# A graph network on one core: four of its five adjacency products in float32r halves, edge weights from rows in SBUF

## The reference

```python
# layer 0, three rounds: sum over neighbours, then two linear layers with batch norms
agg = segment_sum(h[src], dst); z = h + agg; z = z @ W1[i] + b1[i]; ...
# layer 1: mean over row = src, of x[col = dst]
agg = segment_sum(x[col], row) / maximum(deg, 1)
# layer 2: mean over dst, of x[src]
agg = segment_sum(x[src], dst) / clip(deg, 1); h = agg @ W_l.T + b_l + x @ W_r.T
# layer 3: weighted max and weighted mean
w = edge_weight / maximum(segment_sum(edge_weight, dst), 1e-12)[dst]
feat = relu(x @ W_pool + b_pool); neigh = segment_max(feat[src] * w[:, None], dst)
h = relu(normalise(x @ W1_self + neigh @ W1_neigh + b1))
neigh2 = segment_sum(h[src] * w[:, None], dst) / maximum(deg, 1)
out = relu(h @ W2_self + neigh2 @ W2_neigh + b2)
```

## Time and profile before

| what | value |
|---|---|
| median of 3 executions (lowest, highest) | 4459.0 us (4453.96, 4469.67) |
| span of the profiled execution | 4464.1 us |
| PE busy | 3506.4 us, 79% |
| DVE busy | 2050.4 us, 46% |
| ACT busy | 1045.6 us, 23% |
| POOL busy | 2442.1 us, 55% |
| DMA moved | 1224.69 MB |

### The profile page before, as it was taken

One profiled execution on the slowest core, in us unless ns is written; L12 is line 12 of the kernel. 1 busy time (PEld: TensorE's weight loads), 2 busy tenths in 40 slices (PEclk: granted clock), 3 DMA queues, 4 the chain that ended last, 5 costly groups with the idle time before them and its releaser, 6 DMA issues.

```text
span 4464.1 us, 71523 instructions
## 1 busy us (share of the span) xinstructions
PE 3506.4 (79%) x24839; PEld 2663.0 (60%) x24839; DVE 2050.4 (46%) x5883; ACT 1045.6 (23%) x2703; POOL 2442.1 (55%) x2510
## 2 busy tenths in 40 slices
PE   0005878564589997899889998999658998989998
PEld 0004666443457774677667775777447777777776
DVE  6533343344244456878765544000334444444445
ACT  0003555342430002000140003000333333333331
POOL 4777777777303444555404444544177777777750
PEclk9999998787889998999999999999868999999999
DMA  9999999887559999787799997666235677767765
GB/s 368 365 364 359 363 367 343 292 296 261 186 152 339 374 376 310 258 273 265 245 349 366 370 349 256 193 193 194 92 110 186 236 257 244 261 236 268 243 228 188
DMA packets 320171, 1224.69 MB, mean 274 GB/s; under 512 B 98815, under 2 KB 111392, under 8 KB 303353
## 3 DMA queue, kind: packets, MB, share of 16 engines
q1 hardware_dynamic: 143706, 705.58, 44.7%
q10 hardware_dynamic: 96287, 459.59, 27.9%
q0 software_dynamic: 79872, 55.32, 5.2%
HBM read 964.59 MB, written 337.59 MB: 292 GB/s over the span
## 4 chain that ended last, share of the span: by engine, by line
PE 36%; POOL 26%; DMA 17%; issue 12%; DVE 5%; POOLq 1%; ACT 1%; another core or an unknown queue 1%; ACTq 1%; DVEq 0%; SPq 0%
PE PS L507 28%; POOL PAN L387 18%; POOL counts L725 7%; DMA counts<-SSB 7%; DMA BB<-share_rows 6%; DMA counts<-val_slot,idx_slot 2%; PE PS L444 2%; PE PS L1430 2%; DMA PAN<-counts 1%; DVE ST L835 1%; PE PS L486 1%; DVE BB L835 1%; PE PS L450 1%; POOLq L719 1%
## 5 line engine op out<-in xcount | busy, mean ns | idle before, releaser
L751 POOL DMA_INDIRECT shares<-dst_f,spare x832 | 808.8, 972 | 1176.7 <-DMA shares<-dst_f,spare 553.6
L507 PE MATMUL PS<-PAN,HH 125*128 125x375 bf16 x8000 | 1405.7, 297 | 29.7 <-DMA PAN<-counts 15.1
L387 POOL DMA_INDIRECT PAN<-table,src_i x832 | 811.2, 975 | 351.6 <-issue 276.8
L725 POOL DMA_INDIRECT counts<-val_slot,idx_slot x832 | 809.3, 973 | 347.9 <-issue 325.8
L507 PEld LDWEIGHTS PS<-PAN,HH 125*128 125x128 bf16 x8000 | 778.2, 98 | 328.6 <-issue 23.3
L507 PE MATMUL PS<-PAN,XP 125*128 125x375 bf16 (+1 forms) x4000 | 863.1, 297 | 0.0
L444 PE MATMUL PS<-PAN,HH 125*128 125x375 bf16 x2000 | 363.1, 305 | 607.6 <-DMA PAN<-counts 607.6
L444 PEld LDWEIGHTS PS<-PAN,HH 125*128 125x128 bf16 x2000 | 180.2, 101 | 649.2 <-issue 487.8
L507 PEld LDWEIGHTS PS<-PAN,XP 125*128 125x128 bf16 x4000 | 389.2, 97 | 150.9 <-issue 1.6
L646 ACT ACTIVATE X<-PS 125x625 bf16<-125x625 bf16 x500 | 345.1, 692 | 450.1 <-PE PS L450 433.0
L872 DVE TENSOR_REDUCE X<-PAN 125x5 f32<-125x3125 bf16 x100 | 334.3, 3400 | 75.5 <-DMA PAN<-counts 75.3
(11 more groups left out here) (263 smaller groups left out, 3876.4 us busy)
## 6 DMA issues: line engine op xcount, KB each, us to landing
PAN<-counts SPq DMA_DIRECT2D x300, 800.0 KB
counts<-SSB ACTq DMA_DIRECT2D x10, 8000.0 KB, 35.9
shares<-SSB SPq DMA_DIRECT2D x50, 1600.0 KB
PAN<-counts ACTq DMA_DIRECT2D x100, 800.0 KB
shares<-blank ACTq DMA_DIRECT2D x25, 3200.0 KB, 16.9
XP<-shares SPq DMA_DIRECT2D x50, 1600.0 KB
PAN<-shares SPq DMA_DIRECT2D x50, 1600.0 KB
turned<-X ACTq DMA_DIRECT2D x100, 781.2 KB
```

The lines of the kernel that those rows point to most:

```text
L387: nc.gpsimd.indirect_dma_start(out=gbuf[g % 2][:, k, :], out_offset=None, in_=source, in_offset=bass.IndirectOffsetOnAxis(ap=src_i[:, t:t ...
L507: last = nc.tensor.matmul(dense_ps[b][h], xpart[part][0:TN, s * SUBJ + j, :], (turned_tile if scales else panel)[u % NPAN][0:TN, j, lo:lo ...
L725: nc.gpsimd.indirect_dma_start(out=counts_flat, out_offset=bass.IndirectOffsetOnAxis(ap=idx_slot[b][:, k:k + 1], axis=0), in_=val_slot[b][ ...
L751: nc.gpsimd.indirect_dma_start(out=shares_flat, out_offset=bass.IndirectOffsetOnAxis(ap=share_at[:, t:t + 1], axis=0), in_=share[:, t:t + ...
```

## The change

Products 2 to 5 take the node rows as two float32r halves (`XH`, `XL`) instead of three bf16 parts. float32r is a four-byte operand type of PE, and both operands must have it, so each panel is first cast from bf16 into one of three slots (`CX` twice, `CP`; `CB` in product 5), six panels of a chunk by ACT and four by DVE (`ON_DVE`). In product 3 ACT casts tile by tile and sums with it. SP reloads a panel's buffer when its cast is done. A panel is then 5 x 2 x 2 = 20 matmuls, of 376 and 250 columns. The weights come from keys, sources and weights that three DMAs put into SBUF once in the build, as rows with a halo of 63 (`half_key`, `half_w`), by one 127-wide product a column (`dve_share_columns`), beside the build's groups; the broadcasts and `dve_shares` are gone. The scatters no longer wait for PE; they wait once for all weights, and for each half of the edges once for the zeros. The zero slices move: 2 in each chunk of product 2, 5 behind it, none later. Not shown are the two rounds' split into halves, the casts between rows, and the names of slots.

```diff
 PART_AT = {DONE_AT[c] + 2 + d: c * NBLK + d for c in range(NBLK - 1) for d in range(NBLK)}
 ZPARTS = 5
 ZBUILT = 5
-ZEROS_AT = {"dense1": (0,) * 10, "taken1": 5, "dense2": (1,) * 10}
-WEIGH_AT = {1: (0,) + (7, 6) * 4 + (0,), 3: (6,) * 8 + (4, 0)}
+ZEROS_AT = {"dense1": (2,) * 10, "taken1": 5, "dense2": (0,) * 10}
+NCAST = 3
+ON_DVE = (1, 3, 6, 8)
+HALO = 63
+HL = T // 2
+HWIDE = HL + 2 * HALO
+LANE = -(-HL // 3)
+SHARES_FROM = 6
+SHARES_TURN = SHARES_FROM + HL // GT
+FAR = 1000.0
 BN_EPS = 1e-5
 NORM_EPS = 1e-12
 
...
+        def cast_may_start(eng, v):
+            n, u = 1 + v // (NBLK * NSUB), v % (NBLK * NSUB)
+            eng.wait_ge(panel_in[u % NPAN], 16 * (NBLK * NSUB // NPAN * n + u // NPAN + 1))
+            if v >= NCAST:
+                eng.wait_ge(panel_used, NPAN + NBLK * NSUB + v - NCAST + 1)
+
+        def act_casts(act, n, c, subs):
+
+            for s in subs:
+                if s in ON_DVE:
+                    continue
+                v = ((n - 1) * NBLK + c) * NSUB + s
+                cast_may_start(act, v)
+                if n == 2:
+                    for j in range(SUBJ):
+                        last = nc.scalar.activation(cast_tile(v)[:, j, :], cast_source(v)[:, j, :], ACT.Copy,
+                                                    accum_out=sums_at(c, s)[:, j:j + 1])
+                else:
+                    last = nc.scalar.activation(cast_tile(v), cast_source(v), ACT.Copy)
+                last.then_inc(cast_act, 1)
...
+        def dve_casts(dve, n, c, subs):
+
+            for s in subs:
+                if s not in ON_DVE:
+                    continue
+                v = ((n - 1) * NBLK + c) * NSUB + s
+                cast_may_start(dve, v)
+                nc.vector.tensor_copy(cast_tile(v), cast_source(v)).then_inc(cast_dve, 1)
+                if n == 2:
+                    nc.vector.tensor_reduce(out=sums_at(c, s), in_=cast_source(v), axis=AX.X, op=ALU.add
+                                            ).then_inc(panel_summed, 1)
...
+        def add_own_halves(to, tile):
+
+            for t in range(TPB):
+                h, lo = (0, t * TN) if t < 3 else (1, t * TN - HALF)
+                at, first = own_columns(lo)
+                for part in range(2):
+                    last = nc.tensor.matmul(to[h][:, at:at + TN + 1], halves[part][0:TN, tile(t), :],
+                                            ident_r[0:TN, first:first + TN + 1], start=False,
+                                            stop=(part == 1 and t in (2, 4)))
+            return last
...
+                    v = (n - 1) * NBLK * NSUB + u
                     pe.wait_ge(xp_ready, NBLK * n + s + 1)
-                    pe.wait_ge(panel_in[u % NPAN], 16 * (uses * (NBLK // 2) * n + u // NPAN + 1))
+                    pe.wait_ge(*cast_done(v))
                     for j in range(SUBJ):
-                        for part in range(3):
-                            for h, (lo, w) in enumerate(((0, HALF), (HALF, BLK - HALF))):
-                                last = nc.tensor.matmul(dense_ps[b][h], xpart[part][0:TN, s * SUBJ + j, :],
-                                                        (turned_tile if scales else panel)[u % NPAN][0:TN, j, lo:lo + w],
+                        for part in range(2):
+                            for h, (lo, w) in enumerate(((0, HALF + 1), (HALF, BLK - HALF))):
+                                last = nc.tensor.matmul(wide_ps[b][h][:, 0:w], halves[part][0:TN, s * SUBJ + j, :],
+                                                        cast_tile(v)[:, j, lo:lo + w],
                                                         start=(s == 0 and j == 0 and part == 0),
                                                         stop=(not own and s == NSUB - 1 and j == SUBJ - 1
-                                                              and part == 2))
+                                                              and part == 1))
                     last.then_inc(panel_used, 1)
                 if own:
-                    add_own(dense_ps[b], lambda t: slice(c * TPB + t, c * TPB + t + 1)).then_inc(dense_full, 1)
+                    add_own_halves(wide_ps[b], lambda t: c * TPB + t).then_inc(dense_full, 1)
...
+                    act_casts(act, n, c, range(0, 3))
+                    keep_dense(act, n, (c - 1) // 2, (c - 1) % 2)
+                    act_casts(act, n, c, range(3, 6))
                     act_linear_chunk(act, 2 * n, c - 1, ACT.Identity, f"L0_b1_{n}", A)
-                keep_dense(act, n, c // 2, c % 2)
+                    act_casts(act, n, c, range(6, NSUB))
                 if n == 1 and c == 0:
                     store_degrees(act, 0, rin, rin_ready, rin_out)
                     act.wait_ge(xp_ready, 2 * NBLK)
                     act.dma_start(bias_raw, a["bias_rows"]).then_inc(bias_in, 16)
-                    act.wait_ge(unit_rows, 1)
-                    act.dma_start(share_rows[0:1, 128:128 + EP].rearrange("o (g e) -> (o g) e", g=G),
-                                  unit_w).then_inc(share_rows_out, 16)
                 blank_slices(act, ZEROS_AT[f"dense{n}"][c])
                 if n == 2 and c == 0:
                     act.wait_ge(xp_ready, 3 * NBLK)
                     act.dma_start(BB[:, :], a["x_rows"]).then_inc(x_rows_in, 16)
-                if n == 1:
-                    if c == 1:
-                        act.wait_ge(share_rows_out, 16 * 3)
-                    if c == 3:
-                        spread_degrees(act, 0, DEG[:, 0:N], rin_out, rin_spread)
-                    share_loads(act, WEIGH_AT[1][c])
+            keep_dense(act, n, (NBLK - 1) // 2, (NBLK - 1) % 2)
             act_linear_chunk(act, 2 * n, NBLK - 1, ACT.Identity, f"L0_b1_{n}", A)
-            if n == 1:
-                act.wait_ge(kw_used, shares_read((1,)))
             act.sem_inc(lin_src, NBLK)
             if n == 1:
                 blank_slices(act, ZEROS_AT["taken1"])
...
         def pool_shares(pool):
 
-            late = GT * shares_read((1,))
-            need = pool.value_load(zneed_i[0:1, 0:1], min_val=1, max_val=NBLK)
-            for g in range(G):
-                pool.wait_ge(share_ready, g + 1)
-                pool.wait_ge(shares_blank, need)
-                need = pool.value_load(zneed_i[0:1, min(g + 1, G - 1):min(g + 1, G - 1) + 1], min_val=1, max_val=NBLK)
-                for t in range(g * GT, (g + 1) * GT):
-                    if t > 2:
-                        pool.wait_ge(shares_out[t % 3], 16 * (t // 3))
-                    if t >= late:
-                        pool.wait_ge(panel_used, NPAN + 3 * NBLK * NSUB + (t - late) * 2 * NBLK * NSUB // (T - late))
-                    else:
-                        pool.wait_ge(panel_used, NPAN + NBLK * NSUB + NSUB + t * (2 * NBLK - 1) * NSUB // late)
-                    nc.gpsimd.indirect_dma_start(
-                        out=shares_flat, out_offset=bass.IndirectOffsetOnAxis(ap=share_at[:, t:t + 1], axis=0),
-                        in_=share[:, t:t + 1], in_offset=None).then_inc(shares_out[t % 3], 16)
+            need = pool.value_load(zneed_i[0:1, G // 2 - 1:G // 2], min_val=1, max_val=NBLK)
+            pool.wait_ge(share_ready, 1)
+            pool.wait_ge(shares_blank, need)
+            pool.value_load(zneed_i[0:1, G - 1:G], min_val=1, max_val=NBLK)
+            begun = 0
+            for half in range(2):
+                if half:
+                    for b in range(3):
+                        pool.wait_ge(shares_out[b], 16 * ((begun - b + 2) // 3))
+                    pool.wait_ge(shares_blank, NBLK)
+                for r in range(LANE):
+                    for q in range(3):
+                        t = half * HL + q * LANE + r
+                        if q * LANE + r >= HL:
+                            continue
+                        if begun > 2:
+                            pool.wait_ge(shares_out[begun % 3], 16 * (begun // 3))
+                        nc.gpsimd.indirect_dma_start(
+                            out=shares_flat, out_offset=bass.IndirectOffsetOnAxis(ap=share_at[:, t:t + 1], axis=0),
+                            in_=share[:, t:t + 1], in_offset=None).then_inc(shares_out[begun % 3], 16)
+                        begun += 1
...
+        def dve_share_columns(dve, h, q, n):
+
+
+            for k in range(n):
+                lo = q + (h * HWIDE + k)
+                last = nc.vector.scalar_tensor_tensor(
+                    out=share_junk[:, k * 128:k * 128 + 2 * HALO + 1], in0=half_key[:, bass.ds(lo, 2 * HALO + 1)],
+                    scalar=half_key[:, bass.ds(lo + HALO, 1)], in1=half_w[:, bass.ds(lo, 2 * HALO + 1)],
+                    op0=ALU.is_equal, op1=ALU.mult, accum_out=share[:, bass.ds(q + (h * HL + k), 1)])
+            return last
...
+                    if i > 1:
+                        dve_share_columns(dve, 0, ((i + 1) * 2 + b - SHARES_FROM) * GT, GT)
+                if i == 1:
+                    dve.wait_ge(halves_in, 16 * 3)
```

(12 more changed lines are left out.)

485 lines of the change are left out of this document (286 added, 199 removed).

## The result

The changed kernel takes 4249.3 us (median of 4, 4243.96 to 4257.11) against 4457.8 of the kernel before on the same chip: a ratio of 0.953, interval 0.951 to 0.954. The forecast was 4110 with a range of 4020 to 4265. The case forecast as likeliest (A) is the one that came, 139 us later than its sum. The profiled execution spans 4255.1 us.

What follows compares the result with a forecast made beforehand. Before the gather, PE's path (2812) and POOL's scatters (2880) compete; scatters govern, so the gather starts at 2882 and the end is 4115, less 5 for the profiled span: 4110 us, range 4020 to 4265.

Steps and rivals of the forecast that it cites:

- (A): Weight scatters on POOL end after PE's path and set the gather; 4045 to 4225, likeliest 4110 us; chance .46.
- What bounds it: Before the gather: PE's path through five products and POOL's 832 scatters; gather possible at 2812 by PE, 2882 by scatters.
- B: Scatters keep up at 1.6 us or below, so PE's path ends last; 4040 us (4010 to 4060); chance .23.
- The price of a matmul: Products 2 to 5: a float32r matmul costs 134.5 ns like bf16, so 29.05 us a chunk, 28.0 in product 4.
- (D): Rival: float32r streams at float32's 264 ns, or its 250-column half costs far more a column; 4953 us; chance .12.
- (E): Rival: each matmul's weight load binds at 194 ns, 40.9 us a chunk; end 4390 us; chance .08.
- Product 2 held by DMA: Product 2: panels and two zero slices make 14.75 MB a chunk, 41.3 us at 357 GB/s; gain about 1 us a chunk.
- First chunks and rows between: PE's path: first chunks of products 3 to 5 at 50, 45, 40 us; rows between products 41, 43, 34.
- The scatters: POOL, from 1454: 2.2 us each in product 2, 1.4 at lower load, 1.78 steady, 1.3 after product 5; end 2880.
- Rival C: DVE's casts keep POOL from issuing scatters, 1.8 us for each of 120 casts, 216 us lost; end 4268; chance .08.
- The build: Column products on DVE hide under POOL's pace of 10.75 us a group; the build gets 10 us longer (0 to 35).

Runs made afterwards that it cites:

- experiment 1: Changed kernel with six weight scatters allowed to stand out instead of three; 4216.1 us, ratio 0.9455 to the kernel before.
- experiment 2: Changed kernel with the 20 zero slices of product 2 moved to product 3; 4429.7 us.
- experiment 4: Changed kernel with DVE's panel casts in chunks 1 to 9 of each product cut to 13 of 625 columns; 4231.7 us.
- experiments 5 and 6: Changed kernel, slower chip: 5 with matmuls of 314 and 312 columns in product 4, 5570.0 us; 6 with DVE's cast forms swapped between products, 5530.5 us.
- experiment 7: Changed kernel, zeros spread over products 2 and 3, slower chip: three out, median 5568.9 us; six out, degree store behind bias load, 5956.6 and 5953.5 us.

## Why the prediction was right or wrong

**What bounds it: right.** Two paths to the gather, scatters and PE's; the scatters end last (A). PE's path of 4045 was given as 4040 for B; it is 4209 by experiment 1's gather.

**The price of a matmul: right in kind, 8% off.** Not 264 (D) nor 194 (E) but 145 for my 134.5. 200 a chunk make 2.0 us: 31.1 and 30.0 for 29.05 and 28.0. "Both float32 rows look like the same instruction run as two passes" stands with the result, but is not shown by it. The load's row of 194 ns as a length on the load engine came back as 190 to 202, and it bound nothing: at one load each 145 ns, loads overlap too. By the Trainium skill, "TensorE: Matmul & The Clock Gate", section "Step-by-step: what each phase is for", the next weights load while the present matmul runs, and the trace agrees. The 107 ns that the prediction estimated from the Trainium skill is not what it shows; the rows have 190 to 202.

**Product 2 held by DMA: right**, shown by experiment 2. The size was off: 44.2 for 41.3 us, because I spread bytes evenly over the chunk, and two slices come as one burst before the panels (the 21 to 24 us waits; DMA share .92, not .99).

**A term that was missing.** The first chunk of product 2 took 66.7 us for 44. The issue that holds ACT for 21 us is in the trace before as well (its row there reads 23.36 us), hidden, since ACT had nothing due. The change put casts behind it. My text says for every moved step what is queued behind it; this was a step that did not move, and the new work went in behind it.

**First chunks and rows between.** 62, 59 and 57 us for 50, 45 and 40; 57, 32 and 47 between for 41, 47 and 34. That is 43 and 14; with 1.6 to 2.1 us in each of 27 chunks (51), 49 in product 2 and 5 at its start it makes 162 of the 164 us by which PE's path is longer than forecast (2976 for 2812).

**The scatters: the paces that failed.** The gather starts at 3023.1 for 2882, 141 us late. With the forecast's paces, but the measured start of the scatters (29 us late, 21 of it ACT's issue) and the measured lengths of PE's stages, the last scatter would be at 2942 instead of 2880: 62 us come from there. The other 80 are paces. The furthest off is "the rows between and the first chunks, 216 us of lower load, at 1.4": there (1813 to 1875, 2154 to 2246, 2515 to 2619) it was 160 scatters in 257 us, 1.61, which is worth 31 us. 2.47 for 2.2 up to product 3 is 21 (2.38 in product 2, slower in the rows behind it), 1.83 for 1.78 in the steady parts 16, and 1.44 for 1.3 from product 5's end on 12. The 1.4 and the 1.3 leaned on 1.24, which came from taking 118.6 us of waits for PE off a row; but while POOL waits for PE its landings go on, so the row has few landing waits left to show. The nearest to a free rate with three out are the rows between products 4 and 5, 36 scatters from 2514.4 to 2561.8, 1.35 at a DMA share of .16, and the tail.

**Rival C: right as a mechanism, in one product of four.** A DVE cast takes 1.79 us in product 4 (one run of 3125) and 3.41 elsewhere (from five runs), where I took 1.8 for all. The timeline of product 4, then of product 5:

```profile
2288.56 1.82 DVE L470 CAST CX<-PAN 125x3125 fp32r<-125x3125 bf16 x1 [7.96 <-PE PS L594]
2288.56 1.94 POOL L849 DMA_INDIRECT shares<-dst_f,spare  x1 [0.30 <-issue]
...
2686.04 3.41 DVE L470 CAST CB<-PAN 125x3125 fp32r<-125x3125 bf16 x1 [1.58 <-PE PS L594]
2686.26 0.96 POOL L849 DMA_INDIRECT shares<-dst_f,spare  x1 [0.30 <-DMA shares<-dst_f,spare]
```

The fast cast holds a scatter's issue (1.94 for .96), the slow one doesn't. It costs 34 us of POOL's time in product 4, and by experiment 4 all of DVE's casts cost at most 31 us of the end. With six out, where landings don't hide it, it sets the pace of product 4, 1.51 for 1.30 (experiment 1). The Trainium skill's rule on DVE's fast modes and GpSimd ("SBUF — State Buffer", "Who interferes with whom") agrees with these rows.

**The build** pays 16 us (last count scatter at 1185.7 for 1169.8) where 10 were forecast, so the column products are not all hidden under POOL: its waits for DVE's places in the build grew from 21.1 to 83.4 us (L920, L1040), while its idle time without a named cause fell by 50.

**Two sums that don't come out.** 30 x 13.1 + 10 x 1.3 is 406, not 419; with 419 D's bound is 204 ns, not 202. And 153 scatters in 200 us are 10.46 us a group, not 10.75, still above the 10.35 of DVE. Neither moves the forecast.

**Not foreseen at all:** that on a chip of another kind PE crawls beside scatters that run back to back. The wait for PE's progress, which I read as pacing for its own sake, kept them apart. I costed its removal as a gain only. The changed kernel itself was not run there. Its nearest relatives, three out and the same scatters (experiments 5 and 6, one execution each), were 7% slower than the kernel before, and experiment 7's with three out 2.5 to 7%.

## What to carry to other kernels

Before work is put on an engine's queue, read what that queue already stalls on, also where the stall is hidden now. When a rate is taken from a row, ask what was waiting elsewhere meanwhile: a wait taken off does not leave the free rate. A wait that couples a DMA-issuing engine to the consumer is not idle time to be removed for nothing; keep it, place it so that it costs nothing, and measure on more than one chip. When a queue moves little, ask who asks it for so little before calling it blocked.

## What the runs showed of the hardware

- float32r products cost 145 ns for 313 columns at the granted clock of 1.00 (2.4 GHz), bf16 134.5 for 312.5; float32 264.
- A DVE cast from bf16 to float32r of 3125 elements takes 1.79 us as one run, 3.41 from five runs of 625 into one, 2.12 as five of 624. The fast ones (1.79 and 2.12) lengthen POOL's indirect DMA issues beside them from .96 us to as much as 2.6; beside the slow ones none of 234 was lengthened.
- A scatter of 128 values lands such that three out give 1.87 us each at a DMA share of .75 and 1.35 to 1.47 at .15 to .16; six out give 1.30 at .75.
- A DMA issue behind a store of 6250 four-byte pieces stood 21.3 us; ahead of it, .23. Then the next issue, 26 us after the store, stood 9.9.
- On one chip on which the kernel before takes 5155 to 5194 us, scatters issued without a pause, 1.26 to 1.40 us apart, left PE one instruction in 1.40 us (a matmul each 2.8 us, "issue" before it) until 28 to 29 us after the last of them, with three out as with six. With scatters that follow PE's progress, on a second such chip, that didn't come. Where the kernel before takes 4458, the same pace (experiment 1, product 3) left PE 145 ns a matmul. Why is open.
